# A pipelined attention stage: side work dealt over 44 places of a sequence, maxima of four heads turned at once, the value bias added by TensorE

## The chip, the cores and the metric

The kernel runs on one core of one Trainium2 chip. The metric is the device time of one execution in microseconds; lower is better. A core has five engines with a queue of instructions each, taken in order: TensorE (PE, with its weight loads as PEld), VectorE (DVE), ScalarE (ACT), GpSimd (POOL) and SyncE (SP, which here only issues DMAs). They meet at semaphores.

## The reference

Eight sequences of 512 tokens with 128 features pass four layers, each `x = x + layernorm(layer(layernorm(x)))`: a GRU, an expert layer, attention, and a gated feed-forward layer. The edit touches the third:

```python
proj = xn @ W_in.T + b_in
q, k, v, p, y = jnp.split(proj, [D_EXP, 2 * D_EXP, 3 * D_EXP, 4 * D_EXP], axis=-1)
k = (1 - smear) * k + smear * k_prev
pos = jnp.cumsum(jax.nn.sigmoid(y).transpose(0, 2, 1), axis=-1)
mask = causal - (pos[..., :, None] - pos[..., None, :])
scores = jnp.einsum('bhid,bhjd->bhij', q / s, k / s) / np.sqrt(D_HEAD) + mask
attn = jax.nn.softmax(scores, axis=-1)
o = jnp.einsum('bhij,bhjd->bhid', attn, v)
out = jax.nn.silu(p) * o @ W_out.T
return layer_norm(out, out_ln_w, out_ln_b)
```

There are 16 heads of 16 features, D_EXP is 256.

## The kernel before

The four layers run one after another; the attention's block is lines 956 to 1616. Scores are computed twice. Once with queries on partitions: DVE takes their negated maxima (`max_item` L1312 on PE, `reduce_item` L1555 on DVE). Once with keys on partitions and the maxima already in the sum: ACT takes the exponential (`exp_item` L1328 on PE, L1464 on ACT), and PE multiplies by the values (`times_v` L1361). To hold float32 values in bfloat16 operands, q, k, the positions and the maxima are split in three parts each and stacked: QS and KS have 102 rows for every head. POOL splits q and k (`split`, L1200 to L1206), and SyncE stores the parts to DRAM (q_parts L1132, k_extra L1135, k_parts L1143) and loads them as stacks (QS L1140, KS L1146 and L1149), two sequences ahead. A QS load waits until the scores for the exponentials of the sequence that used this buffer are all computed (`e_ps`), and everything behind it in SyncE's queue waits with it.

`sequences` writes the order of every engine by hand. For each sequence b it runs four groups of four heads; a group has four steps j, over 512, 384, 256 and 128 columns of scores, and these hold 4, 4, 2 and 1 items (11 in a group, 44 in a sequence). Each item goes through one of two PSUM banks for each of the two score products. Two groups ahead the maxima are taken (`maxima`), and for the group's maxima DVE splits them in parts (L1566 to L1572), PE turns them into rows (`rows_of_maxima`, L1342, sixteen small transposes of 6 columns) and ACT writes them in QS (L1453, `m_in`). Behind a group come its last value product, the copy OT (L1470), the transposes back (`heads_out`, L1392) and DVE's division (L1584, L1586, `on`).

Side work for other sequences stands in 16 places s (a group's step each): `project_qk` for sequence b+2 in s 10 to 15 (XN transposes L1253, y L1261, the four q and k projections L1268, the cumulative sum L1277, the transposes of its parts KA L1285, copy KAT L1443; K is scaled and smeared on DVE in L1514 and L1516), `project_v` for b+1 in s 7 to 10 (L1299 on PE, bias in VV L1542 and PB L1544 on DVE, tanh L1448, SP L1535), and `output` for b-1 in s 4 to 15 (gating on POOL L1225, transposes L1405, copy GT L1476, W_out L1413, copy T L1481, two layer norms on DVE and POOL). The side matmuls share PSUM banks 6 and 7 with each other. Body 0 and bodies 5 to 7 are written out, bodies 1 to 4 are a loop of two rounds with two bodies each.

## Time and profile before

| what | before |
|---|---|
| median of three runs | 2024.89 us |
| lowest, highest | 2016.74, 2028.94 us |
| profiled execution: its time | 2025.31 us |
| profiled execution: its span, first to last instruction | 2023.2 us |
| PE busy | 1678.1 us, 83% |
| DVE busy | 1207.7 us, 60% |
| ACT busy | 756.5 us, 37% |
| POOL busy | 349.0 us, 17% |
| DMA traffic | 65.58 MB |
| attention's block, first to last instruction | 1268.0 to 1930.6 us |

The busy shares are means over four layers with different limits. The rows below the diff are from the attention's part alone. In a timeline row stand the start in us from the span's start, the length in us, the engine and line, what is written and read, how many instructions are merged, and in brackets how long the engine had been idle before and what ended it. The busy end of a matmul is modelled, so the distance between the starts of neighbours is the better measure of what a group of matmuls takes.

### The profile page before, as it was taken

How to read it: one execution, taken by the hardware profiler on the slowest of the kernel's cores; microseconds unless marked ns; L12 is line 12 of the kernel's file. 1: busy time of each engine (PE TensorE's matmuls, PEld its weight loads, DVE VectorE, ACT ScalarE, POOL GpSimd, SP SyncE). 2: the span in 40 equal slices, each digit the busy share in tenths (PEclk: the TensorE clock that was granted, in tenths of full speed). 3: DMA queues.
4: the chain of work that ended last, by engine and by line, in shares of the span. 5: the costliest groups of instructions: out<-in, count | busy, mean ns of one | idle time of the engine just before them, and what ended most of it. 6: DMA issues, size and time to landing. Idle time of an engine off the chain costs nothing. (4 is left out here: it accounts for less than half of the span.)

```text
span 2023.2 us, 65356 instructions
## 1 busy us (share of the span) xinstructions
PE 1678.1 (83%) x24995; PEld 1273.6 (63%) x24995; DVE 1207.7 (60%) x5630; ACT 756.5 (37%) x2596; POOL 349.0 (17%) x546
## 2 busy tenths in 40 slices
PE   3877777899999999999999988358888788788757
PEld 2366767788888888888888866224444344444423
DVE  4655555666666666666666633546666576676356
ACT  2522222223232323232323222116555455556545
POOL 3000000000000000000000022620332142231244
PEclk6955555555555555555555555659999899889979
DMA  5000000000000000000000000292652643652001
GB/s 115 0 18 16 18 16 18 18 17 16 16 16 18 16 16 16 16 16 16 16 16 16 16 3 0 36 141 29 91 78 37 84 73 42 83 78 21 1 6 37
DMA packets 99299, 65.58 MB, mean 32 GB/s; under 512 B 30830, under 2 KB 98950, under 8 KB 99206
## 3 DMA queue, kind: packets, MB, share of 16 engines
q1 hardware_dynamic: 95094, 63.79, 18.2%
q8 instruction: 58, 0.95, 0.2%
q10 hardware_dynamic: 4112, 0.55, 0.2%
q14 instruction: 35, 0.29, 0.1%
HBM read 31.77 MB, written 15.47 MB: 23 GB/s over the span
## 5 line engine op out<-in xcount | busy, mean ns | idle before, releaser
L672 PE MATMUL PS<-G,W 128*128 128x8 f16 x18432 | 580.2, 169 | 92.8 <-DVE G L845 88.5
L672 PEld LDWEIGHTS PS<-G,W 128*128 128x128 f16 x18432 | 545.9, 105 | 171.4 <-DVE G L845 145.5
L776 ACT ACTIVATE tr<-PS 128x16 f32<-128x16 f32 x512 | 94.2, 184 | 550.3 <-PE PS L672 550.3
L1555 DVE TENSOR_REDUCE MX<-PS 128x1 f32<-128x512 f32 (+3 forms) x352 | 213.6, 639 | 133.0 <-PE PS L1315 121.2
L831 DVE SCALAR_TENSOR_TENSOR u_<-tr,PS 128x16 f32<-128x16 f32 x512 | 87.8, 171 | 256.8 <-PE PS L672 247.5
L1464 ACT ACTIVATE PT<-PS 128x512 f32<-128x512 f32 (+1 forms) x352 | 186.2, 557 | 96.7 <-PE PS L1331 92.6
L1312 PE MATMUL PS<-KS,QS 99*128 99x256 bf16 (+3 forms) x512 | 142.7, 330 | 46.9 <-DVE MX L1555 32.5
L1328 PE MATMUL PS<-QS,KS 102*128 102x256 bf16 (+3 forms) x512 | 139.0, 323 | 49.7 <-ACT PT L1464 27.2
L678 PE MATMUL PS<-XS,ident 128*128 128x64 f32 x516 | 172.3, 438 | 5.6 <-DMA XS<-XI 5.6
L778 ACT ACTIVATE tz<-PS 128x16 f32<-128x16 f32 x512 | 94.2, 184 | 192.5 <-PE PS L672 192.5
L643 POOL TENSOR_TENSOR rt<-mv,eps 128x1 f32<-128x1 f32 x96 | 18.4, 192 | 706.2 <-DVE mv L866 706.2
L839 DVE SCALAR_TENSOR_TENSOR zg<-tz,HR 128x16 f32<-128x16 f32 x512 | 89.7, 175 | 74.8 <-ACT tz L778 68.9
L678 PEld LDWEIGHTS PS<-XS,ident 128*128 128x128 f32 x516 | 129.8, 312 | 6.8 <-issue 4.4
L1328 PEld LDWEIGHTS PS<-QS,KS 102*128 102x128 bf16 x512 | 45.0, 102 | 119.5 <-ACT PT L1464 58.5
L780 ACT ACTIVATE n_<-v_ 128x16 f32<-128x16 f32 x512 | 110.6, 216 | 9.6 <-DVE v_ L835 9.6
L1312 PEld LDWEIGHTS PS<-KS,QS 99*128 99x128 bf16 x512 | 45.9, 103 | 92.7 <-DVE MX L1555 56.3
L750 PE MATMUL PS<-LAT,lbT 32*128 32x128 f32 x256 | 101.4, 497 | 0.0
L835 DVE TENSOR_TENSOR v_<-u_,XS 128x16 f32<-128x16 f32 x512 | 90.7, 177 | 17.5
L852 DVE TENSOR_TENSOR G<-HR,G 128x16 f16<-128x16 f32 x512 | 89.6, 175 | 17.5
L1453 ACT ACTIVATE QS<-PS 6x512 bf16<-6x512 bf16 x128 | 75.2, 588 | 66.2 <-PE PS L1342 63.8
L845 DVE SCALAR_TENSOR_TENSOR G<-zg,zn 128x16 f16<-128x16 f32 x512 | 89.4, 175 | 17.6
L746 PE MATMUL PS<-XFT,wiT 128*128 128x128 f32 x256 | 96.7, 481 | 0.8 <-ACT INT L805 0.5
(272 smaller groups left out, 2778.6 us busy)
## 6 DMA issues: line engine op xcount, KB each, us to landing
XS<-XI SPq DMA_DIRECT2D x130, 96.0 KB, 1.9
QS<-q_parts SPq DMA_DIRECT2D x48, 256.0 KB
KS<-k_parts SPq DMA_DIRECT2D x48, 256.0 KB
q_parts<-PQ SPq DMA_DIRECT2D x16, 384.0 KB, 2.6
k_parts<-PK SPq DMA_DIRECT2D x16, 384.0 KB, 12.8
HS<-HR SPq DMA_DIRECT2D x128, 32.0 KB, 1.7
X<-in_L_attn_x_dram SPq DMA_DIRECT2D x8, 256.0 KB, 7.3
out_dram<-X SPq DMA_DIRECT2D x8, 256.0 KB, 2.3
```

What stands on the lines that cost most here:

```text
L672: return pe.matmul(bank[:, p, o:o + B], W[:, kc, w:w + P], G[:, kc, :], start=False, stop=True, skip_group_check=True)
L678: return pe.matmul(gates[gate][0][:, p, 0:U * NSTEP], ident[:, :], src, start=True, stop=False, skip_group_check=True)
L746: pe.matmul(p_base[c], wiT[:, c * P:(c + 1) * P], XFT[:, :], start=True, stop=False)
L750: pe.matmul(p_base[c], lbT[:, c * P:(c + 1) * P], LAT[:, :], start=False, stop=True).then_inc(base.sem, 1)
L776: act.activation(tr[:, :], pR[:, p, o:o + NSTEP], ACT.Tanh, scale=gate_scale).then_inc(hn_tr.sem, 1)
L778: act.activation(tz[:, :], pZ[:, p, o:o + NSTEP], ACT.Tanh, scale=gate_scale).then_inc(tz_ready.sem, 1)
L780: act.activation(n_[:, :], v_[:, :], ACT.Tanh, scale=n_scale).then_inc(n_ready.sem, 1)
L835: dve.tensor_tensor(v_[:, :], u_[:, :], XS[:, p, k, 4:6, :].rearrange("p c b -> p (c b)"), ALU.add).then_inc(v_ready.sem, 1)
L1312: pe.matmul(bank[:, a * w:(a + 1) * w], QS[0:KM, p, 4 * g + i, q], KS[0:KM, p, 4 * g + i, 0:w], start=(a == 0), stop=False, skip_group_che ...
L1328: pe.matmul(bank[:, a * w:(a + 1) * w], KS[0:KF, p, 4 * g + i, j * P:(j + 1) * P], QS[0:KF, p, 4 * g + i, j * P:S], start=(a == 0), stop=F ...
L1464: act.activation(PT[:, j % 2, heads[0]:heads[-1] + 1, 0:w], p_e[:, k % 2, 0:len(heads) * w].rearrange("p (a w) -> p a w", w=w), ACT.Exp).t ...
L1555: dve.tensor_reduce(MX[:, heads[0]:heads[-1] + 1, NT - 1 - it], p_x[:, k % 2, 0:len(heads) * w].rearrange("p (a w) -> p a w", w=w), AX.X, ...
```

## The change

The 16 places become 44, one behind each item, and each side operation is put in a place of its own: `project_qk` for b+2 in slots 0 to 19, `output` for b-1 in slots 10 to 43 (POOL's gating 10, ON's transposes 17 and 20 with the two halves now in the other order, W_out 22 and 23, copy T 24, norms 25 to 43), `project_v` for b+1 in slots 24 to 32. In a group's slots k = 0 to 10: the last value product of the group behind at 0, copy OT at 1, transposes back at 3, division at 4 and 5. The maxima are split in parts at k 0 to 3 of the following group, one operation a slot; they are turned at k 6 and copied in QS at 7 to 10, one head a slot. Each of the group's first four exponential items waits for its own head's row alone. MX, XT and ON get a second buffer.

QA is now padded to 32 columns a head, so that four transposes of all 128 columns stand for sixteen. The bias of v and p is no longer added by DVE: its three bfloat16 parts lie in the first three rows of `bv3`, and a matmul with a matrix of ones adds it to the projection in PSUM. PB is gone; VV is a copy, and tanh and SP read PSUM. Seven DVE operations ahead of `x_moments` make `bv3`. In the prelude group 0's rows are made ahead of group 1's maxima.

The diff, cut to its core:

```diff
-            PB = sb(ctx, "PB", [P, 2, DE])
+            bv3 = sb(ctx, "bv3", [P, 2 * DE], BF16)
+            onesw = sb(ctx, "ones_w", [P, P], BF16)
             TH = sb(ctx, "TH", [P, 2, DE])
-            MX = sb(ctx, "MX", [P, 4, NT])
+            MX = sb(ctx, "MX", [P, 2, 4, NT])
             MR = sb(ctx, "MR", [P, 4, NT])
-            QA = sb(ctx, "QA", [P, 4, NT, 6], BF16)
+            QA = sb(ctx, "QA", [P, NT, 4, 32], BF16)
             OT = sb(ctx, "OT", [P, S])
             RS_ = sb(ctx, "RS_", [P, NT, 4])
-            ON = sb(ctx, "ON", [P, NT, HEADS, DH])
+            ON = sb(ctx, "ON", [P, 2, NT, HEADS, DH])
...
-            def sequences(eng, project_qk, project_v, maxima, rows_of_maxima, slot, values_late, heads_out, output):
+            def sequences(eng, item, max_parts, values_late, heads_out, rows_of_maxima, output, project_v, project_qk, maxima):
 
                 def start():
-                    for s in range(10, 16):
-                        project_qk(0, 0, s)
-                    for s in range(7, 11):
-                        project_v(0, 0, s, None)
-                    for s in range(10, 16):
-                        project_qk(1, 1, s)
-                    for g in range(2):
-                        for j in range(NT):
-                            maxima(0, 0, g, j)
-                    rows_of_maxima(0, 0, 0, None)
+                    for i in range(SLOTS):
+                        project_qk(0, 0, i)
+                    for i in range(SLOTS):
+                        project_v(0, 0, i, None)
+                    for i in range(SLOTS):
+                        project_qk(1, 1, i)
+                    for j in range(NT):
+                        for n in range(len(ITEMS[j])):
+                            maxima(0, 0, 0, j, n)
+                    for k in range(NI):
+                        max_parts(0, 0, 0, k)
+                        rows_of_maxima(0, 0, 0, k, None)
+                    for j in range(NT):
+                        for n in range(len(ITEMS[j])):
+                            maxima(0, 0, 1, j, n)
 
                 def body(b, p, before, after, after2):
...
-                            s = NT * g + j
-                            slot(b, p, g, j, group(g + 2), group(g - 1))
-                            if j == 0 and group(g - 1):
-                                values_late(*group(g - 1))
-                            if j == 1 and group(g + 1):
-                                rows_of_maxima(*group(g + 1), group(g - 2) if g >= 2 or before is not None else None)
-                            if j == 3 and group(g - 1):
-                                heads_out(*group(g - 1), group(g + 1))
-                            if before is not None:
-                                output(before, 1 - p, s)
-                            if after is not None and 7 <= s <= 10:
-                                project_v(after, 1 - p, s, before)
-                            if after2 is not None and s >= 10:
-                                project_qk(after2, p, s)
+                            for n in range(len(ITEMS[j])):
+                                k = FIRST[j] + n
+                                i = NI * g + k
+                                item(b, p, g, j, n, group(g + 2))
+                                if group(g + 1):
+                                    max_parts(*group(g + 1), k)
+                                if group(g - 1):
+                                    values_late(*group(g - 1), k)
+                                    heads_out(*group(g - 1), k)
+                                if group(g + 1):
+                                    rows_of_maxima(*group(g + 1), k, group(g - 1))
+                                if before is not None:
+                                    output(before, 1 - p, i)
+                                if after is not None:
+                                    project_v(after, 1 - p, i, before)
+                                if after2 is not None:
...
-                values_late(7, 1, 3)
-                heads_out(7, 1, 3, None)
-                for s in range(4, 16):
-                    output(7, 1, s)
+                for k in range(NI):
+                    values_late(7, 1, 3, k)
+                    heads_out(7, 1, 3, k)
+                for i in range(SLOTS):
...
-                def project_qk(b, p, s):
-                    for i in {12: (0,), 13: (1,), 14: (2,), 15: (3,)}.get(s, ()):
-                        split(b, i)
+                def project_qk(b, p, i):
+                    for c in {6: (0,), 8: (1,), 12: (2,), 14: (3,)}.get(i, ()):
+                        split(b, c)
...
-                    for c in {12: (0,), 13: (1, 2), 14: (3,)}.get(s, ()):
+                    for c in {4: (0,), 6: (1,), 7: (2,), 8: (3,)}.get(i, ()):
...
+                    for t in {10: (0, 1), 11: (2,), 12: (3,)}.get(i, ()):
+                        if t == 0:
+                            pe.wait_ge(qk.sem, qk.value(pe, b, 3))
+                            pe.wait_ge(sg.sem, sg.value(pe, b))
...
+                    for t in {24: (0,), 26: (1,), 28: (2,), 30: (3,)}.get(i, ()):
+                        if t == 0:
+                            if before is None:
+                                pe.wait_ge(ka.sem, ka.value(pe, 2 * b))
+                            else:
+                                pe.wait_ge(gT.sem, gT.value(pe, before))
+                        if t == 1:
+                            if before is None:
+                                pe.wait_ge(kaT.sem, kaT.value(pe, 2 * b))
+                            else:
+                                pe.wait_ge(t_kept.sem, t_kept.value(pe, before))
+                        if t >= 2:
+                            pe.wait_ge(sp_.sem, sp_.value(pe, b, t - 1))
+                        bank = PS[:, 7 - t % 2, :]
+                        pe.matmul(bank, XT[:, p, t * P:(t + 1) * P], winT[:, 2 * DE:4 * DE], start=True, stop=False)
+                        pe.matmul(bank, onesw[:, :], bv3[:, :], start=False, stop=True).then_inc(vp_ps.sem, 1)
 
...
-                def rows_of_maxima(b, p, g, in_use):
-
-                    pe.wait_ge(qa.sem, qa.value(pe, b, 5 * (g + 1)))
-                    if in_use:
-                        pe.wait_ge(on.sem, on.value(pe, in_use[0], in_use[2] + 1))
-                    for i in range(4):
+                def rows_of_maxima(b, p, g, k, in_use):
+                    if k == 6:
+                        pe.wait_ge(qa.sem, qa.value(pe, b, 5 * (g + 1)))
+                        if in_use:
+                            pe.wait_ge(on.sem, on.value(pe, in_use[0], in_use[2] + 1))
                         for t in range(NT):
-                            last = pe.transpose(p_m.bitcast(BF16)[32 * i:32 * i + 6, t * P:(t + 1) * P], QA[:, i, t, :],
-                                                identb[:, :], tile_position=(0, 32 * i))
-                    last.then_inc(m_ps.sem, 1)
...
-                    if j >= 1:
-                        if j == 1 and behind:
-                            pe.wait_ge(o_kept.sem, o_kept.value(pe, behind[0], behind[2] + 1))
+                        pe.wait_ge(m_in.sem, m_in.value(pe, b, 4 * g + n + 1))
+                    exp_item(b, p, g, j, n)
+                    if ahead:
+                        maxima(*ahead, j, n)
+                    if j >= 1 and n == len(ITEMS[j]) - 1:
+                        if j == 1:
+                            if g == 0:
+                                pe.wait_ge(vv.sem, vv.value(pe, b))
+                            if not (isinstance(b, int) and b == 0 and g == 0):
+                                pe.wait_ge(o_kept.sem, o_kept.value(pe, b, g))
                         times_v(b, p, g, j - 1)
 
...
+                def values_late(b, p, g, k):
+                    if k == 0:
+                        times_v(b, p, g, NT - 1).then_inc(o_ps.sem, 1)
+
+                def heads_out(b, p, g, k):
+                    if k == 3:
+                        pe.wait_ge(o_kept.sem, o_kept.value(pe, b, g + 1))
+                        if not (isinstance(b, int) and b == B - 1 and g == NG4 - 1):
+                            pe.wait_ge(m_in.sem, m_in.value(pe, b, 4 * (g + 2)))
+                        else:
+                            pe.wait_ge(on.sem, on.value(pe, b, g))
+                        for t in range(NT):
+                            last = pe.transpose(p_m[:, t * P:(t + 1) * P], OT[:, t * P:(t + 1) * P], ident[:, :])
+                        last.then_inc(oT_ps.sem, 1)
...
+                    for c in {17: (1,), 20: (0,)}.get(i, ()):
+                        if c == 1:
+
+                            pe.wait_ge(gated.sem, gated.value(pe, b))
+                        if not (isinstance(b, int) and b + 3 > B - 1):
+                            after = b + 3 if isinstance(b, int) else pe.snap(b + 3)
+                            done = ka if c else kaT
+                            pe.wait_ge(done.sem, done.value(pe, after))
+                        else:
+                            pe.wait_ge(sp_.sem, NT * min(b + 2, B))
+                            if b == B - 1:
+                                pe.wait_ge(t_kept.sem, t_kept.value(pe, b - 1))
+                        for t in range(NT):
+                            last = pe.transpose(PS[:, 6 + c, t * P:(t + 1) * P],
+                                                ON[:, p, t, 8 * c:8 * c + 8, :].rearrange("p h d -> p (h d)"), ident[:, :])
+                        last.then_inc(gT_ps.sem, 1)
+                    for half in {22: (0,), 23: (1,)}.get(i, ()):
                         pe.wait_ge(gT.sem, gT.value(pe, b))
...
+                    for t in {25: (0,), 27: (1,), 29: (2,), 31: (3,)}.get(i, ()):
+                        act.wait_ge(vv.sem, vv.value(act, b, t + 1))
+                        act.activation(TH[:, t % 2, :], PS[:, 7 - t % 2, DE:], ACT.Tanh, scale=0.5).then_inc(pth.sem, 1)
...
+                    if k >= 7:
+                        i = k - 7
+                        act.wait_ge(m_ps.sem, m_ps.value(act, b, g + 1))
...
+                dve.tensor_copy(bvp[:, 0, :], bvpy[:, 0:2 * DE]).then_inc(bv.sem, 1)
+                dve.tensor_tensor(bvr[:, 0, :], bvpy[:, 0:2 * DE], bvp[:, 0, :], ALU.subtract).then_inc(bv.sem, 1)
+                dve.tensor_copy(bvp[:, 1, :], bvr[:, 0, :]).then_inc(bv.sem, 1)
+                dve.tensor_tensor(bvp[:, 2, :], bvr[:, 0, :], bvp[:, 1, :], ALU.subtract).then_inc(bv.sem, 1)
+                dve.tensor_scalar(bvr[:, 0, :], bvp[:, 0, :], ident[:, 0:1], None, ALU.mult).then_inc(bv.sem, 1)
+                dve.scalar_tensor_tensor(bvr[:, 1, :], bvp[:, 1, :], ident[:, 1:2], bvr[:, 0, :], ALU.mult, ALU.add).then_inc(bv.sem, 1)
+                dve.scalar_tensor_tensor(bv3[:, :], bvp[:, 2, :], ident[:, 2:3], bvr[:, 1, :], ALU.mult, ALU.add).then_inc(bv.sem, 2)
...
+                    for t in {25: (0,), 27: (1,), 29: (2,), 31: (3,)}.get(i, ()):
+                        if t == 0 and before is not None:
+                            dve.wait_ge(gated.sem, gated.value(dve, before))
+                        dve.wait_ge(vp_ps.sem, vp_ps.value(dve, b, t + 1))
+                        dve.tensor_copy(VV[:, p, t, :, 0:DH], PS[:, 7 - t % 2, 0:DE].rearrange("p (h d) -> p h d", d=DH)).then_inc(vv.sem, 1)
+                    for t in {26: (0,), 28: (1,), 30: (2,), 32: (3,)}.get(i, ()):
                         dve.wait_ge(pth.sem, pth.value(dve, b, t + 1))
-                        dve.scalar_tensor_tensor(SP[:, p, t, :], TH[:, t % 2, :], 1.0, PB[:, t % 2, :], ALU.add, ALU.mult).then_inc(sp_.sem, 1)
...
+                def max_parts(b, p, g, k):
+                    part = lambda r: QA[:, :, :, r].rearrange("p t i -> p i t")
+                    mx = MX[:, g % 2, :, :]
+                    if k == 0:
```

## Rows read from the trace of the kernel before

**Rows 1.** Timeline, ScalarE: start, length, operation; OT copies of last groups.

```profile
1429.02 0.60 ACT L1470 ACTIVATE OT<-PS 128x512 f32<-128x512 f32 x1 [0.55 <-PE PS L1361]
...
1584.52 0.60 ACT L1470 ACTIVATE OT<-PS 128x512 f32<-128x512 f32 x1 [0.55 <-PE PS L1361]
...
1803.31 0.60 ACT L1470 ACTIVATE OT<-PS 128x512 f32<-128x512 f32 x1 [0.55 <-PE PS L1361]
...
1864.90 0.60 ACT L1470 ACTIVATE OT<-PS 128x512 f32<-128x512 f32 x1
...
1907.09 0.60 ACT L1470 ACTIVATE OT<-PS 128x512 f32<-128x512 f32 x1 [0.94 <-PE PS L1361]
```

**Rows 2.** Timeline, PE: the first exponential scores, idle time before in brackets.

```profile
1361.32 0.61 PE L1328 MATMUL PS<-QS,KS 102*128 102x512 bf16 x1 [2.58 <-ACT QS L1453]
```

**Rows 3.** Busy time of each engine in body 3, clock, DMA share, GB/s.

```profile
core 0: us, PE busy (x) PEld busy (x) DVE busy (x) ACT busy (x) POOL busy (x), PEclk, DMA share, GB/s
1584.52:1653.91 69.39, 58.62 (x541) 33.50 (x540) 48.25 (x119) 41.52 (x78) 21.97 (x24) 0.94 0.35 54
```

**Rows 4.** Timeline, SyncE's queue: issues of the loads for sequence 6.

```profile
1722.09 2.83 SPq L1140 DMA_DIRECT2D QS<-q_parts  x6
...
1740.29 2.81 SPq L1149 DMA_DIRECT2D KS<-k_parts  x6
```

**Rows 5.** Busy times in a 3 us stretch after the load's end.

```profile
1755.00:1758.00 3.00, 1.18 (x5) 0.65 (x6) 0.00 (x0) 0.46 (x1) 0.00 (x0) 0.50 0.01 1
```

**Rows 6.** Timeline, PE: first score matmul of halves, idle before in brackets.

```profile
1756.82 0.59 PE L1328 MATMUL PS<-QS,KS 102*128 102x512 bf16 x1 [5.43 <-issue]
...
1831.86 0.38 PE L1328 MATMUL PS<-QS,KS 102*128 102x512 bf16 x1 [4.40 <-issue]
...
1861.45 0.38 PE L1328 MATMUL PS<-QS,KS 102*128 102x512 bf16 x1
```

**Rows 7.** Timeline, PE: side work in the last group of body 4.

```profile
1703.07 1.06 PE L1261 MATMUL PS<-winT,XT 128*128 128x16 f32 x8
...
1708.56 1.98 PE L1268 MATMUL PS<-XT,winT 128*128 128x512 f32 x4
...
1710.38 0.38 PE L1328 MATMUL PS<-QS,KS 102*128 102x256 bf16 x2
...
1713.55 0.29 PE L1277 MATMUL PS<-SG,tri 128*128 128x16 f32 x2
...
1715.70 0.38 PE L1328 MATMUL PS<-QS,KS 102*128 102x128 bf16 x4
...
1720.00 0.66 PE L1285 MATMUL PS<-identb,KA 128*96 128x128 bf16 x4 [2.08 <-DVE KA L1528]
```

**Rows 8.** Timeline, DVE: last reduces of two light groups, and the loop's jump.

```profile
1581.34 1.29 DVE L1555 TENSOR_REDUCE MX<-PS 128x1 f32<-128x512 f32 x2 [9.69 <-issue]
...
1661.96 0.69 DVE L1555 TENSOR_REDUCE MX<-PS 128x4 f32<-128x512 f32 x1 [2.15 <-PE PS L1315]
...
1674.03 0.69 DVE L1555 TENSOR_REDUCE MX<-PS 128x4 f32<-128x512 f32 x1 [2.15 <-PE PS L1315]
```

**Rows 9.** Timeline, PE: two items, output and value work.

```profile
1546.62 0.38 PE L1328 MATMUL PS<-QS,KS 102*128 102x512 bf16 x1
...
1547.17 0.38 PE L1328 MATMUL PS<-QS,KS 102*128 102x512 bf16 x1
...
1745.45 1.09 PE L1405 MATMUL PS<-ident,ON 128*128 128x128 f32 x8
...
1748.57 1.95 PE L1413 MATMUL PS<-waoT,GT 128*128 128x128 f32 x16
...
1750.36 1.02 PE L1299 MATMUL PS<-winT,XT 128*128 128x512 f32 x2
```

**Rows 10.** Groups by line and form: count, busy us, mean ns, idle before.

```profile
L1544 DVE TENSOR_TENSOR PB<-PS,bvpy 128x256 f32<-128x256 f32 x32 | 13.3, 415 | 0.0
L1514 DVE TENSOR_SCALAR KK<-KF_,qsc 128x512 f32<-128x512 f32 x16 | 10.1, 631 | 0.0
```

**Rows 11.** One line's instructions: count, minimum/median/maximum ns.

```profile
L1568 DVE TENSOR_TENSOR MR<-MX,QA x32: 178/180/1089, 1350.2 to 1885.5; 128x16 f32<-128x16 f32 x32
```

329 lines of the change are left out of this document (153 added, 176 removed).

## The prediction

> **What bounds the kernel now.** I call the work between two sequences' last OT copies a body, numbered by the sequence whose exponentials it computes, and a group a quarter of it (four heads). I first read when ScalarE copies OT for the last group of a sequence [rows 1]: body 0 lasts from the first exponential at 1361.3 [rows 2] to 1429.0, 67.7 us; bodies 1 and 2 together take 155.5; bodies 3 to 5 together 218.8 (72.9 each); body 6 61.6; body 7, which has no maxima ahead, 42.2. That is 545.8 us of the 2023.2 us span, and the edit touches only this stage. Then I read the busy times of one body [rows 3]: PE 58.6 of 69.4 us, DVE 48.3, ACT 41.5, POOL 22.0. PE is the nearest to full, and 10.8 us of a body it does nothing.
>
> The third view is SyncE and PE around the load of the stacks. For sequence 6 the first QS load is issued at 1722.09, the KS loads at 1740.29 [rows 4], by 1755 the DMA engines are at 0.01 [rows 5], and PE goes on at 1756.82 after 5.43 us without work [rows 6]. So the chain QS in, k_parts out, KS in takes about 32.5 us, and 34.7 us from the issue to the first matmul behind it. Other sequences show the same, with waits of four to five microseconds in bodies 4, 5 and 6 (body 6: 4.40 [rows 6]). This is a gate: the first half of a body can't be shorter than this chain. After such an idle stretch PE's granted clock reads 0.50, the 1.2 GHz level [rows 5], and the next matmuls take nearly twice as long.
>
> The fourth is PE in the last group of body 4 [rows 7]. The K and Q projection stands there in five lumps, PE then waits 2.08 us for DVE's KA parts at 1720.00, and from 1703.07, some way into the group, to its end at 1720.4 it takes 17.3 us where a whole group without such work takes 12.07 (DVE's last reduce at 1661.96 to the next at 1674.03 [rows 8]). So the loss has two places: the lumps at the end of a body, and the DMA gate in its middle.
>
> **The change, part by part.** Light group: 12.07 us, less the 1.09 of the ON transposes that lie in it [rows 9], 11.0.
>
> Side work that moves. The K and Q projection goes from the last third (s 10 to 15) to slots 0 to 20. On PE it is: XN transposes about 0.5 (as KA's), y 1.0, four projections at 1.82 for two, 3.6, the cumulative sum 1713.55 to 1715.70, 2.15, KA transposes 0.4 [rows 7]: 7.6 us in all, and the ON transposes, 1.1, stay in this half. First half: 2 x 11.0 + 7.6 + 1.1 = 30.7 us. The moved operations' handovers now each have a slot (about 1.4 us) between producer and consumer. Four look tight: XT at slot 3 for y at 4, KA at 16 (two DVE operations in one slot) for the ON transposes at 17, `on` at 5 for the maxima rows at 6, KAT at 19 for slot 20. At 0.5 us each I put 2 us: 32.7. The floor by the gate: the QS load waits for the last exponential scores of the body before (e_ps), which PE issues about 1.5 us before the body ends once the lumps are gone, so 34.7 - 1.5 = 33.2, or less by the slower first matmul. Both limits are almost the same; I take 33 for the first half. Today it is 36.4 in body 5 (1720.4 to 1756.8).
>
> Second half: two light groups 22.0, value projection four times 0.91, 3.6, W matmuls 1748.57 to 1750.36, 1.8 [rows 9], and the bias matmuls. A bf16 matmul of 512 columns with one of 128 behind it follows every 0.275 us (1546.62 and 1547.17, two such pairs [rows 9]), so 0.22 for the 512 columns; at most half a float32 pair, 0.45. Four a body: 0.9 (bound 1.8). Sum 28.3. Check: body 6 has this same side work without the K and Q lumps, and its second half runs 1831.86 to 1861.45, 29.6 us [rows 6], part of it at 1.2 GHz. I take 28.8. Today it is some 38 with the lumps.
>
> Body: 33 + 28.8 = 61.8.
>
> The other engines. DVE loses four PB additions, 4 x 0.415 = 1.7 us [rows 10], and the VV addition becomes a copy of the same size; 48.3 - 1.7 = 46.6 stays under 61.8. The maxima's splitting moves from the end of the group that made them to the next group's slots 0 to 3, behind the four 512-wide reduces (0.65 each, two in 1.29 [rows 8]): 4 x 0.65 + 0.8 = 3.4 us against PE's 4 x 0.55 + about 0.9 there. So DVE sets those slots, and 0.3 us of PE's side work per group lies free under it; I count nothing for it. ScalarE's tanh now waits for VV and reads PSUM: both belong to the value part's slots, where PE with two float32 passes is the longer; hidden. Without that cover it is 4 x 0.4 us a body, by the PB row. The maxima's sixteen small transposes a group become four of 128 rows: four of about this size take PE 0.4 us or so (KA transposes [rows 7]), the sixteen can't be under nothing; the work is small both ways, so zero, between -0.4 and +0.4 a group, of which DVE covers the cost. Waits per head on m_in are satisfied half a group earlier: nothing. SyncE's order is untouched; q_parts of the next sequence now queue behind the KS loads rather than before, and nobody needs them before the body's end: nothing, and if it did count, 3 us a body. PE's clock: fewer waits over 2 us should leave it at 2.4 GHz; it is inside the half figures.
>
> The jump back of the loop, between bodies 2 and 3: DVE stands 9.69 us for no releaser [rows 8], and bodies 1 and 2 together take 9.7 more than two of 72.9, although no wait of the gate is as long there. The instructions are still as many, so the fetch stays; some of it lies over the gate. I count 12.
>
> Prelude. Seven dependent DVE operations on 512 columns stand ahead of x_moments, whose results everything waits for. Nearest row: 0.631 for a tensor_scalar of that size [rows 10], so 7 x 0.6 = 4.2; nothing hides it. In return the maxima rows of group 0 are copied under the maxima of group 1, where PE now waits 2.58 us [rows 2]; the split that PE then waits for costs 1.5 of it. Net +3.2; between +2 and +6.
>
> **Sum**, against this execution. Body 0 has low-clock first matmuls and no output work: 60, saves 7.7. Bodies 1 to 5: 5 x 61.8 + 12 = 321 against 374.3, saves 53.3. Body 6 has no K and Q work, so the gate alone holds its first half, 33.2, plus 2 for the clock after a long idle stretch, plus 28: 63, costs 1.4. Body 7: lightly dealt, saves 2. The tail is the same chain: nothing. 7.7 + 53.3 - 1.4 + 2 = 61.6, less 3.2 = 58.4. 2023.2 - 58.4 = 1964.8 span; the execution's time is 2.1 over its span: **1967 us**. The median of the three shown, 2024.9, is within 0.4 of this execution's 2025.3.
>
> **The rivals.** (a) PE has no waits but the gate. Second half 28.3 less what lies under DVE in slots 0 to 3 (0.3 to 0.9 a group) and the clock at 2.4 GHz throughout, 26.5; first half 32; no fetch stall. 58.5 x 5 saves 16 more, the fetch 12: 1939. For it: the 1.2 GHz stretches inside the present halves. Against: the light group itself has waits, its last reduce stands 2.15 us for PE [rows 8], and DVE is only 70% busy over a body [rows 3].
>
> (b) DVE and POOL in each other's way. The splitting's subtraction takes 0.18 us, and 1.09 at its longest of 32 [rows 11]; the long ones lie beside POOL's work. Now POOL splits K and Q in slots 6 to 18 and DVE splits maxima in 11 to 14, scales K in 9 to 12 and KA in 14 to 16, all of them ahead of a reduce that PE waits for. Eight operations at up to 0.9 more, 7 us a body in the worst case, half of it likely on the path: 3.5 x 6 = 21, and the first half passes the gate: 1988. The Trainium skill, "SBUF — State Buffer", section "Who interferes with whom", says that a VectorE instruction with two SBUF inputs and a GpSimd one that reads SBUF exclude each other for the whole instruction; the minimum and maximum of that row agree with it. By the rule each such pair would be paid in full, by the median of the row none.
>
> (c) Slower. PE's queue is in order, and every slot now holds one of its side operations with a wait on DVE or ACT, which themselves stand behind that slot's reduce or exponential. If the one-slot distance does not cover the latency, each handover shows: about 20 a body on PE. A body of 3 to 5 takes 72.9 now, so above (72.9 - 61.8)/20 = 0.55 us each it decides, over and above what is counted. At 0.9 a body is 80: 5 x 80 + 12 = 412 against 374.3, bodies 0 and 6 add 5 each, the prelude 3: 2023 + 51 + 2 = 2076. For it: the KA wait of 2.08 is such a handover [rows 7]. Against: it has no work between, and three DVE operations on its chain.
>
> (d) No change: the waits saved at the body's end come back in the first half, because the gate is longer when loads run against more traffic, 40 instead of 34.7, and the second half keeps 31. Body 71, 5 x 71 + 12 = 367, saves 7; with body 0's 3 less and the prelude's 3 more: 2018.
>
> **Numbers.** Forecast 0.6, (a) 0.14, (b) 0.13, (c) 0.06, (d) 0.07. The forecast's own bounds are 1945 to 1985: bias matmuls +0.9 a body and prelude +3 upward, handovers at zero downward. The range, 1938 to 1998, takes in (a) and (b) and leaves out (c), (d) and the ends. A measurement of this kernel can tell about 1% from no change: faster by more (under 2004.6) 0.88, within 0.07, slower 0.05.
>
> **What the later profile would show.** Right: OT copies of last groups 61 to 63 us apart; PE's wait for KA gone; PE's wait at the 23rd slot 0 to 3 us in bodies 1 to 5 and some 8 in body 6; DMA chain still 32 us. Wrong: a first half much over 34 with no wait for KS (handovers or POOL), the subtraction's mean near 1 us (b), or the chain over 36 (d). What would break it most is a fetch stall in more bodies, 10 us each.

## The result and the profile after

The changed kernel takes 2000.3 us, median of four runs (1998.7 to 2005.4), against 2023.8 us for the kernel before in the same session (2016.7 to 2028.9): ratio 0.9881, 95% interval 0.9853 to 0.9909. The profiled execution spans 1997.7 us (2023.2 before). The forecast was 1967 us in a range of 1938 to 1998: the direction is right, the gain is 23.5 us where 58 were forecast, and the time lies just above the range. Of the 25.5 us by which the profiled spans differ, 2.2 are not the edit's: this execution reached the attention's block 2.2 us earlier. The two rows are VectorE's first instruction of the block, before and after:

```profile
1268.07 0.16 DVE L1486 TENSOR_TENSOR bqs<-bqk,qsc 128x2 f32<-128x2 f32 x1 [0.31 <-PEq L495]
```

```profile
1265.90 0.16 DVE L1513 TENSOR_TENSOR bqs<-bqk,qsc 128x2 f32<-128x2 f32 x1 [0.31 <-PEq L495]
```

ScalarE's OT copies of the last groups, timeline of the changed kernel, the counterpart of [rows 1]:

```profile
1427.08 0.59 ACT L1498 ACTIVATE OT<-PS 128x512 f32<-128x512 f32 x1
...
1493.36 0.59 ACT L1498 ACTIVATE OT<-PS 128x512 f32<-128x512 f32 x1
...
1572.88 0.59 ACT L1498 ACTIVATE OT<-PS 128x512 f32<-128x512 f32 x1
...
1640.06 0.59 ACT L1498 ACTIVATE OT<-PS 128x512 f32<-128x512 f32 x1
...
1707.89 0.59 ACT L1498 ACTIVATE OT<-PS 128x512 f32<-128x512 f32 x1
...
1776.61 0.59 ACT L1498 ACTIVATE OT<-PS 128x512 f32<-128x512 f32 x1
...
1841.08 0.59 ACT L1498 ACTIVATE OT<-PS 128x512 f32<-128x512 f32 x1
...
1882.75 0.60 ACT L1498 ACTIVATE OT<-PS 128x512 f32<-128x512 f32 x1 [0.55 <-PE PS L1378]
```

The distances are the bodies. The first exponential scores stand at 1362.8.

| part | before | forecast | after |
|---|---|---|---|
| first exponential scores at | 1361.3 | +3.2 | 1362.8 (+1.5) |
| from the block's first DVE instruction to those scores | 93.25 | +3.2 | 96.94 (+3.7) |
| body 0 | 67.7 | 60 | 64.2 |
| bodies 1, 3, 4, 5, mean | 72.3 | 61.8 | 67.5 |
| body 2, with the loop's jump | 85.1 | 73.8 | 79.5 |
| body 6 | 61.6 | 63 | 64.5 |
| body 7 | 42.2 | 40.2 | 41.7 |

The miss is 5.7 us in the mean of bodies 1 to 5 (4.5 in body 1, 6.9 in body 5), 28.5 us together, and 4.2 in body 0; the rest is small and of both signs. So the question is a body of 67.5 us. These are the four groups of body 4 in the changed kernel, from one OT copy to the next (busy times by stretch, columns as in [rows 3]), and the sum over the 16 groups of bodies 1, 3, 4 and 5:

```profile
1640.06:1659.65 19.59, 16.98 (x139) 10.04 (x137) 11.77 (x27) 12.07 (x24) 10.40 (x11) 1.00 1.05 139
1659.65:1679.08 19.43, 16.52 (x134) 9.85 (x134) 11.15 (x24) 10.50 (x20) 7.22 (x8) 0.82 0.68 100
1679.08:1695.58 16.50, 15.74 (x126) 8.28 (x125) 12.31 (x37) 10.62 (x22) 2.40 (x3) 1.00 0.00 1
1695.58:1707.89 12.31, 10.91 (x106) 5.61 (x104) 10.50 (x30) 8.77 (x18) 3.58 (x5) 1.00 0.16 28
...
sum 270.01, PE 241.09 PEld 135.33 DVE 182.72 ACT 168.21 POOL 93.72; mean PE 15.07 PEld 8.46 DVE 11.42 ACT 10.51 POOL 5.86
```

The second half is 16.50 + 12.31 = 28.8 us, as forecast. The first half is 39.0 here (37.5 to 39.9 in the four bodies) where 33 were forecast. A body holds 7.2 us without PE work, (270.0 - 241.1) / 4, and in this body's group 1 the granted clock is 0.82. PE's waits over the attention stage (who waited, for whom, us in total, times, longest):

```profile
PE PS L1361 <- DVE ON L1628: 21.6, 30, 1.0
PE PS L1332 <- DVE MX L1588: 9.1, 22, 0.7
PE PS L1332 <- DMA KS<-k_parts: 8.7, 1, 8.7
...
PE PS L1269 <- DVE XN L1542: 7.7, 6, 1.9
PE PS L1426 <- DVE KA L1570: 5.5, 5, 1.2
```

The wait for ON in front of the maxima rows comes 30 times, in every group; the waits for XN and KA once a body. On the timeline of PE in body 4:

```profile
1642.15 0.66 PE L1269 MATMUL PS<-ident,XN 128*128 128x128 f32 x4 [1.79 <-DVE XN L1542]
...
1665.48 0.44 PE L1361 MATMUL PS<-identb,QA 128*128 128x128 bf16 x4 [0.73 <-DVE ON L1628]
...
1667.00 1.11 PE L1426 MATMUL PS<-ident,ON 128*128 128x128 f32 x4 [1.07 <-DVE KA L1570]
```

The last two lie 1.5 us apart, and at this place the clock falls, as the stretches of 3 us show:

```profile
1662.00:1665.00 3.00, 1.65 (x11) 0.66 (x10) 3.00 (x10) 1.47 (x3) 2.41 (x4) 1.00 1.14 119
1665.00:1668.00 3.00, 1.44 (x9) 1.17 (x10) 2.18 (x5) 0.00 (x0) 2.71 (x3) 0.61 1.17 125
1668.00:1671.00 3.00, 3.00 (x15) 0.75 (x14) 0.56 (x1) 1.67 (x3) 0.00 (x0) 0.50 0.99 258
1671.00:1674.00 3.00, 3.00 (x28) 2.02 (x26) 1.29 (x2) 1.85 (x4) 0.00 (x0) 0.75 0.05 15
```

In the first two stretches PE is idle about half of the time, while DVE has 3.00 and 2.18 of 3.00 us busy beside a busy POOL. Then PE runs at 0.50, the 1.2 GHz level: 15 matmuls in 3 us. The granted clock of group 1 is under 1.00 in all of bodies 0 to 5 (0.80, 0.91, 0.82, 0.91, 0.82, 0.91). The chain of loads, which the prediction called a gate, is not the cause of the long first half. SyncE's queue for sequence 5:

```profile
1637.29 2.83 SPq L1154 DMA_DIRECT2D QS<-q_parts  x6
...
1654.88 2.81 SPq L1163 DMA_DIRECT2D KS<-k_parts  x6
```

DMA share is down to 0.05 in 1671 to 1674, 34 us after the issue, and PE waits for KS in none of these bodies.

### The profile page after: what moved, and what is told of

Read it like the earlier page. It is cut to its first block and busy times, and to the rows that moved or that the text cites. A ratio compares the mean times of both kernels' runs of the same rounds, so it can differ in the third digit from the quotient of the medians.

```text
span 1997.7 us, 64778 instructions
## 1 busy us (share of the span) xinstructions
PE 1679.8 (84%) x24643; PEld 1273.2 (64%) x24643; DVE 1188.4 (59%) x5605; ACT 758.6 (38%) x2596; POOL 352.3 (18%) x547
## 3 DMA queue, kind: packets, MB, share of 16 engines
q1 hardware_dynamic: 95094, 63.79, 18.6%
## 5 line engine op out<-in xcount | busy, mean ns | idle before, releaser
L1588 DVE TENSOR_REDUCE MX<-PS 128x1 f32<-128x512 f32 (+3 forms) x352 | 223.0, 636 | 194.4 <-PE PS L1335 192.7
L1491 ACT ACTIVATE PT<-PS 128x512 f32<-128x512 f32 (+1 forms) x352 | 193.9, 559 | 176.2 <-PE PS L1351 172.5
L1332 PE MATMUL PS<-KS,QS 99*128 99x256 bf16 (+3 forms) x512 | 136.2, 318 | 32.5 <-DMA KS<-k_parts 20.8
L1348 PE MATMUL PS<-QS,KS 102*128 102x256 bf16 (+3 forms) x512 | 132.6, 311 | 4.5 <-issue 3.0
L1378 PE MATMUL PS<-PT,VV 128*32 128x512 f32 (+3 forms) x1024 | 101.5, 467 | 8.3 <-issue 7.7
L757 PE MATMUL PS<-woT,INT 128*128 128x128 f32 x256 | 93.3, 477 | 0.0
```

Source lines behind the costliest of these rows:

```text
L1332: pe.matmul(bank[:, a * w:(a + 1) * w], QS[0:KM, p, 4 * g + i, q], KS[0:KM, p, 4 * g + i, 0:w], start=(a == 0), stop=False, skip_group_che ...
L1348: pe.matmul(bank[:, a * w:(a + 1) * w], KS[0:KF, p, 4 * g + i, j * P:(j + 1) * P], QS[0:KF, p, 4 * g + i, j * P:S], start=(a == 0), stop=F ...
L1378: last = pe.matmul(p_o[32 * i:32 * i + 32, j * P:S], VV[:, p, j, 4 * g + i, :], PT[:, j % 2, i, 0:S - j * P], start=(j == 0), stop=(j == N ...
L1491: act.activation(PT[:, j % 2, heads[0]:heads[-1] + 1, 0:w], p_e[:, k % 2, 0:len(heads) * w].rearrange("p (a w) -> p a w", w=w), ACT.Exp).t ...
L1588: dve.tensor_reduce(MX[:, g % 2, heads[0]:heads[-1] + 1, NT - 1 - it], p_x[:, k % 2, 0:len(heads) * w].rearrange("p (a w) -> p a w", w=w), ...
```

## The experiments

Three theories for the 5.7 us. *Handovers*: PE waits at places where the producer stands one slot ahead; the forecast gave this 2 us a body. *Contention*, rival (b): DVE's small operations are stretched beside POOL's splits, and PE waits for them. *More PE work*: the side operations cost more than summed; then neither edit helps. "A body" below is the mean of bodies 1, 3, 4 and 5, 67.5 us in the changed kernel. Where no interval is given, the time is a single run. The runs come from several sessions, in which the kernel before took between 2023.8 and 2031.3 us, so a difference of two whole times from different sessions holds only to some 7 us. The groups are the finer measure: groups 2 and 3 of a kernel repeat from body to body within 0.1 us where the clock reads 1.00, groups 0 and 1 mostly within 1 us. A table at the end of this section has the stage's length for every run.

### POOL's splits cut to a sliver

```diff
+                    w = S if isinstance(b, int) and b < 2 else 8
-                    pool.tensor_copy(dst[:, c, 0, :], src[:, c, :]).then_inc(parts.sem, 1)
+                    pool.tensor_copy(dst[:, c, 0, 0:w], src[:, c, 0:w]).then_inc(parts.sem, 1)
```

and so for all four operations of a split.

> POOL's sixteen split operations a sequence work on 8 of 512 columns from sequence 2 on (K and Q parts of the rest keep what stood there, so the output of sequences 2 to 7 is not the reference's); all waits, issues and loads stay. Contention theory (rival b): DVE's small operations beside POOL's splits (the QA cast 509 ns in the mean against 207 before, the KA cast 748 against 394) made PE wait in slots 9 to 18, so groups 0 and 1 of bodies 1 to 5 fall from 19.6 and 19.0 us to about 18.5 and 16.8, bodies by 3.3, the time by 17 to about 1983. Handover theory: the DVE operations get short again but PE still waits for the one-slot handovers; below 1 us a body, 1995 to 1999. More-PE-work theory: no change, 2000.

1979.3 us, ratio 0.9768 [0.9735, 0.9801]: 21 us less than the changed kernel. Groups 0 and 1 of body 4, then the sum over bodies 1, 3, 4, 5:

```profile
1625.09:1645.92 20.83, 18.41 (x140) 11.11 (x137) 11.52 (x28) 12.18 (x24) 5.03 (x14) 0.92 1.04 139
1645.92:1660.68 14.76, 13.71 (x134) 8.70 (x134) 8.84 (x23) 10.46 (x20) 0.79 (x4) 1.00 0.79 118
...
sum 257.35, PE 236.43 PEld 133.63 DVE 171.45 ACT 168.01 POOL 46.61; mean PE 14.78 PEld 8.35 DVE 10.72 ACT 10.50 POOL 2.91
```

Group 1 fell from 19.43 to 14.76, its clock is 1.00; group 0 did not gain, and group 3 took 13.9 us instead of 12.3 in bodies 4 and 5. PE's wait for KA went from 5.5 to 1.0 us, those for reduces from 9.1 to 1.9, those for ON and XN stayed (21.8 and 8.2). DVE's durations, per source line (count, minimum/median/maximum ns), the changed kernel and then this one:

```profile
L1554 DVE TENSOR_SCALAR KK<-KF_,qsc x16: 474/792/1387, 1299.0 to 1729.3; 128x512 f32<-128x512 f32 x16
L1568 DVE CAST KA<-PR x8: 542/770/805, 1302.3 to 1734.8; 128x64 bf16<-128x64 f32 x8
```

```profile
L1555 DVE TENSOR_SCALAR KK<-KF_,qsc x16: 477/484/1401, 1298.7 to 1709.6; 128x512 f32<-128x512 f32 x16
L1569 DVE CAST KA<-PR x8: 258/262/1058, 1301.9 to 1715.0; 128x64 bf16<-128x64 f32 x8
```

So contention is real, and its price is about that of rival (b): 21 us.

Group 3 in this kernel says something on the clock. These are 3 us of body 3 and the same 3 us of body 4:

```profile
1616.29:1617.79 1.50, 0.51 (x7) 0.28 (x6) 1.50 (x7) 0.46 (x1) 0.00 (x0) 1.00 0.00 0
1617.79:1619.29 1.50, 1.50 (x15) 0.39 (x12) 1.19 (x7) 1.08 (x2) 0.60 (x2) 1.00 0.00 0
...
1680.68:1682.18 1.50, 0.51 (x7) 0.27 (x6) 1.50 (x7) 0.47 (x1) 0.00 (x0) 1.00 0.00 0
1682.18:1683.68 1.50, 1.50 (x11) 0.54 (x12) 1.31 (x7) 0.98 (x2) 0.59 (x2) 0.55 0.04 11
```

PE had done the same work with the same waits (0.3 us for a reduce, then 1.0 for ON in both), and the clock stayed at 1.00 once and fell to 0.55 once. The edit adds no wait there. So short waits are not always followed by a fall; what decides it at such a place is open.

### Two waits mended

```diff
-                    if k == 6:
+                    if k == 7:
...
-                    if k >= 7:
-                        i = k - 7
+                    for i in {8: (0,), 9: (1,), 10: (2, 3)}.get(k, ()):
...
-                            pe.wait_ge(done.sem, done.value(pe, after))
+                            pe.wait_ge(done.sem, done.value(pe, after, 2) if c else done.value(pe, after))
```

The first is PE's turn of the maxima's parts, the second ScalarE's copies of the heads' rows. The ON transposes of the second column write PSUM bank 7, which holds the cumulative sum; DVE reads that for the last time in KA's second operation, while the kernel waits for all five counts.

> Two handovers of the changed kernel get more distance, nothing else: the maxima's rows are turned at item 7 of a group instead of 6, and the ON transposes of the second column wait for the second of the five counts of KA, which frees their bank, not for the fifth. Handover theory: PE's waits for ON at the maxima rows (21.6 us over the stage) and for KA at the ON transposes (5.5) go, and most of that is time: 1978, groups 2 and 3 unchanged where they show no wait, group 1 down by 2. Contention theory: DVE is late by a crowd, the next reduce is waited for instead, and 2 to 6 us are won: 1995. If DVE or the next slot's reduce hides the rows wait, the second half (28.8) does not move at all and only the first half gains.

1977.7 us, ratio 0.976 [0.9716, 0.9804]: 22.6 us less than the changed kernel, with POOL as busy as before. Group 1 and the sum:

```profile
1643.91:1659.55 15.64, 13.90 (x134) 8.66 (x134) 11.08 (x24) 10.39 (x21) 7.23 (x8) 1.00 0.84 120
...
sum 252.31, PE 234.05 PEld 132.94 DVE 181.18 ACT 165.85 POOL 93.85; mean PE 14.63 PEld 8.31 DVE 11.32 ACT 10.37 POOL 5.87
```

The waits for ON and KA, 27 us, are gone from the list. PE waits elsewhere instead: for exponentials 5.3 us (1.1 before this edit), for YB 3.7 (none) and for GT 3.2 (0.2). A body is 63.1. Of the 4.4 us that it lost, 2.7 are idle time and 1.8 are PE busy time for the same matmuls, (241.1 - 234.1) / 4, beside a clock of group 1 that went from 0.82 or 0.91 to 1.00. My guess that the second half might not move was wrong: it went from 28.8 to 27.4, since group 3 fell from 12.31 to 11.29 and group 2 from 16.50 to 16.09.

### Only the wait for KA

The last line of the diff above, alone.

> Of the two waits only the second: the ON transposes of the second column wait for the second of the five counts of KA. Its wait is 5.5 us over the stage. Theory that a wait costs its own length: 1995. Theory that the clock falls by the waits together (group 1 of the changed kernel has 0.82 to 0.91, both kernels without one of the causes 1.00): group 1 goes from 18.6 to 19.4 down to 16.5 to 17, 2 to 2.5 us a body with its clock back at 1.00, 1987; the wait for ON stays at some 20 us over the stage, group 2 at 16.50 and group 3 at 12.31.

1985.1 us in a single run, 15 less than the changed kernel (13.9 by the stage's length), for a wait of 5.5 us in total. Group 1 went from 18.6 to 19.4 down to 15.7 to 16.2, groups 2 and 3 stayed at 16.50 and 12.31, as expected. The same stretch of body 4 as above (the body starts 5.7 us earlier here):

```profile
1656.00:1659.00 3.00, 1.91 (x13) 0.67 (x11) 3.00 (x10) 1.47 (x3) 2.46 (x3) 1.00 1.17 110
1659.00:1662.00 3.00, 2.27 (x22) 1.15 (x22) 2.90 (x6) 1.11 (x3) 2.70 (x3) 1.00 1.15 112
1662.00:1665.00 3.00, 2.87 (x35) 1.96 (x32) 1.37 (x3) 2.77 (x5) 0.22 (x1) 1.00 1.11 203
```

DVE and POOL are as crowded, the maxima rows still wait 0.73 us; but PE has work 1 us sooner, the clock stays at 1.00, as it does in group 1 of every body, and 35 matmuls run where 15 ran. A wait of 1.1 us cost about 3. Body 3 is an exception: its group 0 took 22.4 us at clock 0.78, behind the loop's jump.

This run also prices the other wait. From here to the kernel with both waits mended, a body loses 1.8 us more (64.9 to 63.1): 0.2 in group 1, 0.4 in group 2, 1.0 in group 3. The waits for ON that are gone with it are 21.1 us over the stage, about 2.9 a body. So they were worth somewhat over half of their length, and most of it in the second half of the body.

### Both

> Both: the two waits mended and POOL's splits cut to 8 of 512 columns from sequence 2 on (so the output of sequences 2 to 7 is not the reference's). If the stretched DVE operations cost only through the two waits, nothing is left to win over the kernel with two waits mended: 1975 to 1978, group 1 at 15.0 to 15.6. If contention has a price of its own (each reduce that PE waits for, 9.0 us over the stage), groups 0 and 1 lose another 1.5 us a body together: 1968.

1963.7 us in a single run: 36.6 under the changed kernel. The two edits alone gave 21.0 and 22.6, so 7 us of the two are the same (8.4 by the stage's length). They lie in group 1: in the mean of four bodies it is 18.9 us in the changed kernel, 14.9 without the splits, 15.7 with the waits mended and 14.1 with both. Either edit alone takes away most of the wait for KA and the low clock behind it. Group 1 of body 4 is 14.08 (15.64 with the splits), a body 61.4. The first theory in my expectation (contention costs only through the two waits) is wrong: the waits for reduces, 9.0 us with two waits mended, are 2.0 here. Contention has a price of its own, some 1.7 us a body.

### More distance

The two waits, and two steps. The first: `project_qk` one slot later from the XN transposes on. The second: the KA parts one a slot, and all of `output` and `project_v` from slot 17 on two slots later. Of PE's part, the first two pairs of lines are the first step, the rest the second:

```diff
-                    if i == 2:
+                    if i == 3:
...
-                    for c in {4: (0,), 6: (1,), 7: (2,), 8: (3,)}.get(i, ()):
+                    for c in {5: (0,), 7: (1,), 8: (2,), 9: (3,)}.get(i, ()):
...
-                    for t in {24: (0,), 26: (1,), 28: (2,), 30: (3,)}.get(i, ()):
+                    for t in {26: (0,), 28: (1,), 30: (2,), 32: (3,)}.get(i, ()):
...
-                    for c in {17: (1,), 20: (0,)}.get(i, ()):
+                    for c in {19: (1,), 22: (0,)}.get(i, ()):
...
-                    for half in {22: (0,), 23: (1,)}.get(i, ()):
+                    for half in {24: (0,), 25: (1,)}.get(i, ()):
```

> The edit of the run before, and besides the K and Q side work from the XN transposes on one slot later on every engine, the KA parts one operation a slot (15 to 18), and everything behind them two slots later (ON transposes 19 and 22, KA transposes 20, W 24 and 25, values 26 to 32, the output's moments and scaling two later). Handover theory: the XN wait (1.8 us a body) goes as well, group 0 falls from 19.6 to 17.8, group 1 from 19.0 to 17 and its clock stays at 1.0; first half 35 instead of 38.5, the time 1972 to 1980. Gate theory: the stacks now are needed at 35 us after the body's start and the k parts go out one slot later, so the wait for KS comes back, and the first half stays at 38: 1996. Contention theory: POOL's splits still lie on DVE's KK and KA operations: 1990.

1983.3 us, ratio 0.9787 [0.9756, 0.9819]: slower than the two waits alone. It is none of the theories as written. Group 0 gained (19.61 to 18.05, XN's waits 7.3 to 0.2 us in total), but group 2 lost 2.5 in every body:

```profile
1662.09:1680.73 18.64, 16.93 (x135) 9.45 (x132) 12.14 (x37) 10.85 (x24) 1.22 (x2) 1.00 0.00 1
```

The stretches run from one OT copy, at the second slot of a group, to the next; so the W matmuls, at 22 and 23 in group 1's stretch, came at 24 and 25 into group 2's, beside the value projections. PE's busy time there rose by 1.3 (15.63 to 16.93) and the stretch by 2.55, while group 1 is 0.2 to 1.6 shorter than in the next kernel. Waits for reduces rose to 19.7 us. Which of the moved operations makes group 2 longer was not tested. Without this second step:

> The two waits mended (maxima's rows turned at item 7, ON transposes behind KA's second count) and the K and Q side work from the XN transposes on one slot later; nothing behind it moves. If distance is what counts in group 0 and the worse group 2 of the spread kernel (18.64 against 16.09) came from the value, W and moment work being moved two slots, this takes the better half of each: group 0 18.0, group 1 15.6 to 16.5, group 2 16.1, group 3 11.3, a body 61.5, and the time 1970. If the shift itself made DVE's crowd at 10 to 16 worse (POOL's K split beside the KA parts), group 1 goes to 17.3 and the time stays at 1977.

1969.0 us, ratio 0.9697 [0.9669, 0.9725]. Groups 2 and 3 are back at 16.08 and 11.30; group 0 is 17.55, but group 1 rose from 15.64 to 17.49 at clock 1.00, so both halves of the expectation came true. In the trace the later K operations meet POOL's gating and DVE's maxima parts in one place. DVE, and below it POOL, timelines of body 4:

```profile
1636.25 1.45 DVE L1553 TENSOR_SCALAR KK<-KF_,qsc 128x512 f32<-128x512 f32 x1
...
1638.23 1.86 DVE L1600 CAST QA<-MX 128x16 bf16<-128x16 f32 x1
```

```profile
1636.26 1.16 POOL L1221 TENSOR_TENSOR PQ<-RES,PQ 128x512 bf16<-128x512 f32 x1
...
1637.68 2.35 POOL L1240 TENSOR_TENSOR ON<-ON,SP 128x1024 f32<-128x1024 f32 x1 [0.26 <-POOL PQ L1221]
```

A cast of 16 columns, 0.195 us in the median of the kernel before, took 1.86, and ended at 1640.09, 0.06 us behind the end of POOL's gating at 1640.03.

### K's scale on ScalarE

On top of this:

```diff
-                        dve.tensor_scalar(KK[:, c, :], KF_[:, c, :], qsc[:, c:c + 1], None, ALU.mult).then_inc(kk1.sem, 1)
+                        act.activation(KK[:, c, :], KF_[:, c, :], ACT.Copy, scale=qsc[:, c:c + 1]).then_inc(kk1.sem, 1)
```

> The kernel with two waits mended and the shift, and the two multiplications of K by its scale done by ScalarE (behind its own K copies, items 11 and 12) instead of DVE. In the kernel before this edit one of them took 1.45 us on DVE beside a subtraction on POOL that began with it, and DVE reads 12.9 of 17.5 us in group 1. Contention theory: DVE loses about 1.3 to 2 us of crowd in items 10 to 14, PE's waits for reduces (12.1 us over the stage) halve, group 1 goes from 17.5 to 16.2, the time from 1969 to 1963. If it is the maxima's parts and the gating that collide (a cast of 16 columns took 1.86 us there), the crowd only moves: 1967 to 1970.

1963.3 us in a single run. Group 1 is 15.5 to 16.4, group 0 some 0.5 longer than before this edit, a body 61.2, and the sum:

```profile
sum 244.92, PE 229.87 PEld 130.85 DVE 173.01 ACT 169.87 POOL 92.48; mean PE 14.37 PEld 8.18 DVE 10.81 ACT 10.62 POOL 5.78
```

The waits for reduces did not halve (12.1 to 10.6); PE's waits for KA (1.8) are gone and those for GT went from 3.3 to 1.7. On ScalarE one of these operations takes 0.71 to 0.74 us in all sixteen cases. In bodies 1 and 4 PE now waits 0.8 and 0.6 us for KS: the chain of loads is just reached.

### The small terms

The bias's seven DVE operations moved behind the XN operations of sequence 0 (the seven themselves unchanged):

```diff
-                pe.wait_ge(bv.sem, 8)
...
                             if before is None:
+                                if b == 0:
+                                    pe.wait_ge(bv.sem, 8)
...
+                    if i == 2 and isinstance(b, int) and b == 0:
+                        dve.tensor_copy(bvp[:, 0, :], bvpy[:, 0:2 * DE]).then_inc(bv.sem, 1)
```

> Only the seven DVE operations that split the value bias are moved: behind DVE's XN operations of sequence 0, where it waits for y, and PE waits for them at its first value matmul. The step of the prediction (prelude +3.2, of it 4.2 for the chain) expects the first exponential scores 3 to 4 us earlier than 1362.84 and the time 3 to 4 us less, 1996.5. If the start of the stage is set by something else (weights, POOL's constants), nothing moves: 2000.

1997.4 us, ratio 0.9857 [0.9822, 0.9892], 3 us less, as expected in the total. The first exponential scores come 5.2 us earlier (1357.65), more than expected. Counted from the block's first instruction it is 5.7 us (91.3 against 96.9). Body 0 gives 2.9 back (67.1 against 64.2). The changed kernel's DVE timeline shows why the chain is longer than seven times 0.6:

```profile
1265.97 0.69 DVE L1514 CAST PT<-bvpy 128x512 bf16<-128x512 f32 x1
...
1267.42 2.82 DVE L1518 CAST PT<-PT 128x512 bf16<-128x512 f32 x1
...
1273.05 1.64 DVE L127 BATCH_NORM_STATS2 STa<-X 128x6 f32 x8
```

7.1 us instead of 4.2, of which 2.1 is one cast that lay beside POOL's memsets of VV, KA and QA (1267.33 to 1269.95).

The value bias left out:

```diff
-                        pe.matmul(bank, XT[:, p, t * P:(t + 1) * P], winT[:, 2 * DE:4 * DE], start=True, stop=False)
-                        pe.matmul(bank, onesw[:, :], bv3[:, :], start=False, stop=True).then_inc(vp_ps.sem, 1)
+                        pe.matmul(bank, XT[:, p, t * P:(t + 1) * P], winT[:, 2 * DE:4 * DE], start=True, stop=True).then_inc(vp_ps.sem, 1)
```

> The changed kernel without the value bias: neither the seven DVE operations ahead of the moments nor the four bias matmuls a sequence (v and the gate projection get no bias added). The prediction's terms: 0.9 us a body (bound 1.8), all of it in groups 2 and 3, where values are projected, and 4.2 us of the prelude. So group 2 from 16.50 to 15.6, first exponential scores 3 to 5 us earlier than 1362.84 with the body 0 longer by some of it, sum 7.2 + 3 to 4, the time 1989. If the bias matmuls lie under DVE's or ScalarE's part of the value handover, groups 2 and 3 do not move: 1996.

1990.0 us in a single run. Group 2 went from 16.50 to 15.86, so four bias matmuls cost 0.64 us a body where I had 0.9. Group 3 stayed at 12.31, but for bodies 4 and 5, where it took 13.87 at a clock of 0.88. The first scores are at 1356.5.

Sixteen small transposes a group:

```diff
-                            last = pe.transpose(p_m.bitcast(BF16)[:, t * P:(t + 1) * P], QA[:, t, :, :].rearrange("p i r -> p (i r)"), identb[:, :])
+                            for i in range(4):
+                                last = pe.transpose(p_m.bitcast(BF16)[32 * i:32 * i + 6, t * P:(t + 1) * P], QA[:, t, i, 0:6],
+                                                    identb[:, :], tile_position=(0, 32 * i))
```

> The changed kernel with the maxima's rows turned by sixteen small transposes a group instead of four of 128 rows, each writing six rows as in the kernel before. The prediction put this part at nothing, between -0.4 and +0.4 a group: 1987 to 2013 at the bounds, 2000 as its value. If PE's time in that slot is what counts, sixteen cost 12 x 0.06 to 0.1 = 0.7 to 1.2 us a group more, 32 groups, 2020 to 2035.

2007.1 us in a single run; group 2 is 16.66, group 3 12.42: sixteen small transposes cost 0.16 and 0.11 us a group more than four. That is 4 us over 32 groups, inside the bound of 0.4 that I had put. The stage is 4.7 us longer; of the rest of the 7, 2.0 lie ahead of the first exponential scores, 1.2 of them ahead of the attention's block. Most of the loop's jump moved from the last group of body 2 (16.3 us, 24.0 in the changed kernel) to the first of body 3 (31.2 us).

SyncE's queue, the k parts first (`k_parts_out` holds the two stores and their waits), together with the late bias, on the kernel with two waits and the shift:

```diff
+                    if not isinstance(b, int):
+                        k_parts_out()
                     if not (isinstance(b, int) and b < 2):
                         sp.wait_ge(e_ps.sem, sp.snap(b * (NI * NG4) - NI * NG4))
```

> The kernel with two waits mended and the shift, and two edits at places far apart: the bias operations late, as in the earlier run (prelude 5 us earlier, body 0 about 3 longer by its clock), and on SyncE's queue the k parts of sequences 2 to 7 go out ahead of the wait for the body's end, so that QS and KS load one behind the other. Gate theory of the prediction (chain QS in, k parts out, KS in sets the first half of body 6): body 6's wait for KS falls from 10.9 us to between 4 and 7, bodies 1 to 5 do not move, since they have no wait there: 1969 - 5 - 2 = 1962. If the DMA engines' bytes alone set the chain (1.0 of share in group 0), the wait falls by 3 at most: 1965.

1965.2 us in a single run. PE's wait for KS in body 6, changed order:

```profile
1774.13 0.61 PE L1339 MATMUL PS<-KS,QS 99*128 99x512 bf16 x1 [4.76 <-DMA KS<-k_parts]
```

10.9 became 4.8, and body 6 went from 63.9 to 61.0. The chain itself got shorter by less than the wait. These are the issue of the QS loads for it without and with the edit, and the matmul behind the wait without it:

```profile
1743.08 2.83 SPq L1154 DMA_DIRECT2D QS<-q_parts  x6
...
1777.28 0.61 PE L1332 MATMUL PS<-KS,QS 99*128 99x512 bf16 x1 [10.88 <-DMA KS<-k_parts]
```

```profile
1742.26 2.83 SPq L1162 DMA_DIRECT2D QS<-q_parts  x6
```

From issue to matmul it is 34.2 us without and 31.9 with the edit, 2.3 less. The rest of the shorter wait is PE itself, which had more to do ahead of it: 15.9 us busy in that group where it had 14.1, and another 2.0 us of waiting. So the k parts' way out was 2 to 3 us of the chain, as the expectation's second theory had it, and the chain is what sets body 6. Bodies 4 and 5 did not move (62.4 and 62.2); bodies 1 to 3 lost 1.3 to 2.3 each, two by a lower clock in group 1 (0.82, 0.91) and one at the loop's jump. Why the clock fell there is open.

### All that helped

Two waits, the shift, K's scale on ScalarE, the bias late, the k parts early:

> All edits that helped, together: two waits mended, K and Q side work one slot later, K's scale on ScalarE, value bias split behind XN of sequence 0, k parts out ahead of the wait for the body's end. If they add: the kernel with the scale on ScalarE took 1963.3; the bias late brought the first exponential scores 5.8 us earlier, the earlier k parts took 2.9 from body 6: 1954 to 1957, bodies 1 and 3 to 5 at 61.2. If a fetch stall in the loop grows again (one more of 2 us was seen with the k parts early), 1958 to 1961.

1955.3 us over five runs (1953.0 to 1957.2), ratio 0.9632 [0.9616, 0.9647], 45 us under the changed kernel and the fastest here. Its longest waits of PE are those for reduces:

```profile
PE PS L1339 <- DVE MX L1595: 9.4, 18, 0.9
```

All kernels, by their profiled execution. The prelude runs from the block's first DVE instruction to the first exponential scores, the stage from there to the last OT copy; "a body" is the mean of bodies 1, 3, 4 and 5.

| kernel | time | prelude | stage | a body |
|---|---|---|---|---|
| before | 2023.8 | 93.3 | 545.8 | 72.3 |
| changed | 2000.3 | 96.9 | 519.9 | 67.5 |
| no splits | 1979.3 | 97.6 | 499.1 | 64.3 |
| only the wait for KA | 1985.1 | 97.5 | 506.0 | 64.9 |
| two waits | 1977.7 | 97.6 | 494.4 | 63.1 |
| two waits, no splits | 1963.7 | 97.8 | 482.0 | 61.4 |
| more distance, both steps | 1983.3 | 97.1 | 501.2 | 64.7 |
| more distance, first step | 1969.0 | 97.9 | 487.9 | 62.3 |
| and K's scale on ScalarE | 1963.3 | 98.2 | 483.0 | 61.2 |
| bias late | 1997.4 | 91.3 | 522.3 | 67.5 |
| no value bias | 1990.0 | 89.9 | 517.3 | 69.7 (jump in body 3) |
| sixteen transposes | 2007.1 | 97.8 | 524.6 | 70.4 (jump in body 3) |
| first step, k parts early, bias late | 1965.2 | 90.8 | 489.2 | 62.9 |
| all that helped | 1955.3 | 90.9 | 478.3 | 61.6 |

## Why the prediction was wrong, step by step

**The PE work was right.** I summed 30.7 us for the first half. With the handovers and DVE's crowd mended (K's scale on ScalarE), PE is busy 30.6 us in body 4's first half (16.76 + 13.87), and a whole body takes 61.2, where the forecast had 61.8. That the two agree so closely is in part luck. The first half of that kernel takes 33.9 in the mean where 33 were forecast, the second 27.4 where 28.8 were. And it needed edits that the changed kernel does not have. So the forecast was near the time of this schedule with its handovers mended: 1963 to 1969, not 2000.

**The step that failed is the handovers.** I named four tight ones (XT, KA, `on`, KAT) and put 0.5 us each, 2 us a body. Mending them step by step took a body from 67.5 to 64.9 (KA), 63.1 (`on`), 62.3 (XN and those behind it, one slot later) and 61.2 (K's scale off DVE): 6.3 us. Three things were wrong with the term:
- Price. KA's wait, 1.1 us a body, cost about 3, since the clock fell behind it in the changed kernel and did not with the wait gone. I had put the clock under "fewer waits over 2 us should leave it at 2.4 GHz"; here waits of 0.73 and 1.07 us, 1.5 us apart, with DVE busy behind them, came ahead of the fall. This is the largest single part. It is not a rule for every wait: those for `on` were worth somewhat over half of their length, since PE then waited for other things.
- Count. `on` at slot 5 for the rows at 6 is no handover of a body but of a group: 30 waits, 21.6 us, 0.72 each, about 2.9 a body. I had counted it once, and in the first half only. In the second half it cost 1.4 us, which my 28.8 hid by being 1.4 too large elsewhere (a value read off body 6, and 0.9 for the bias matmuls that cost 0.64).
- The list. The longest single one, XN at slot 1 for the transposes at 2 (1.79 us in body 4), wasn't on it. KAT and XT, which were, cost little (XT 1.3 us over the stage, KAT does not appear). And KA's wait asks for more than the bank needs, which the changed code says and I didn't read: it waits for five counts where two would do.

**Rival (b) happened, on top.** Contention was worth 21 us by its experiment and 21 by its sum, though by other operations than I had named, so the equal number is luck. The forecast itself had put it at nothing. The Trainium skill, "SBUF — State Buffer", section "Who interferes with whom", has the pair blocked for the whole instruction; the cast of 1.86 us that ends 0.06 us behind POOL's gating agrees with that, and so roughly does the 2.82 us one beside the memsets, which ends 0.3 us behind the third of them. The section also extends it to casts and `tensor_scalar` with one SBUF input in a two-port mode, which I had not drawn on; whether these operations ran in such a mode no trace here shows. I looked at the subtraction with two inputs, whose mean moved little (321 to 358 ns, kernel before to after). The operations that stretched were the cast of KA (416 to 770 ns in the median), the KK `tensor_scalar` (476 to 792) and the QA cast (195 to 306). I had handovers and contention as alternatives; they overlap. From 1963.7, with neither the splits nor the two waits, the splits alone add 14.0 (1977.7), the waits alone 15.6 (1979.3), both 36.6, which is 7 more than 14.0 + 15.6. Where they meet is group 1: of these four kernels only the changed one, with both the splits and the wait for five counts, has a long wait for KA and a low clock there.

**Rival (c)** had the right mechanism at under a third of its price: not 0.9 at twenty places of a body but 0.7 at four (the rows), 1.1 at one (KA) and some 1.3 at one (XN), 5.3 us against 18.

**Rival (d) and the gate.** The chain kept its 34 us, and no body of the middle waits for it, as their first halves are 37 us and more. With the first half at 33.9 PE waits for it by 0.6 to 0.8 us in two bodies, so the floor of 33.2 was about right. Body 6: wait of 8.7 us (some 8 forecast), body 64.5 (63).

**The loop's jump** was right: body 2 is 12.3 us over its neighbour body 3 (12 forecast). It moves with the code: in two of the kernels run most of it stood in group 0 of body 3 instead.

**Prelude.** From the block's first instruction to the first exponential scores it grew by 3.7 us, 3.2 forecast; the +1.5 of the first scores' position holds the 2.2 us by which this execution reached the block earlier. The two terms were both too small and nearly cancel: the kernels with the chain of seven operations take 96.9 to 98.2 us, those without it 89.9 to 91.3, so it costs 6 to 7 and not 4.2. The kernels with the bias late (90.8 to 91.3) are 2 to 2.4 us under the kernel before, where I had 1 for the rows made early; no run isolates that part. **The sixteen transposes** were zero as forecast (0.1 to 0.2 a group). **Body 0** went to 64.2, not 60: it has the same waits, and its later mending (60.3 with two waits, 57.9 at last) shows the forecast was once more that of a schedule without them.

## What to carry to other kernels

When side work is dealt out one operation a slot, list every handover with its distance and *how often it comes*, those that repeat in each group first, and read which count of the semaphore a reused buffer truly needs; moving one consumer by one slot and one wait by three counts was worth as much as the whole change. A wait's length is not its price: on the nearly full engine one of 1.1 us was worth 3, since the clock fell with it, and thirty of 0.72 us were worth about half of their sum, since others took their place. So mend the waits one at a time and read the group's length and clock, not the sum of waits. And when an operation is moved beside a busy GpSimd, look at the casts and one-input `tensor_scalar` operations of VectorE, not only at those with two inputs; ScalarE did the same work in 0.71 to 0.74 us each time.

## What was not expected of the hardware

- Two waits of PE of 0.73 and 1.07 us, 1.5 us apart, were followed by a granted clock of 0.50, the 1.2 GHz level; with the second of them gone it stayed at 1.00 there. In another kernel the same matmuls with the same waits were followed by 1.00 in one body and by 0.55 in the next.
- One DVE cast of 16 columns took 1.86 us beside a POOL multiplication of 2.35, against 0.195 in the median where the splits were cut; one of 512 columns took 2.82 beside POOL memsets, though a memset reads nothing.
- Six loads of 256 KB and two stores of 384 KB share the same queue: with the stores issued before, the chain from the first load's issue to the matmul behind the last one took 31.9 us instead of 34.2.
